# Two norms of a sum moved from VectorE to ScalarE, and the clamp in one pass, in the front stage of a two-layer megakernel

## The chip, the cores and the metric

One Trainium2 chip; the kernel is one program on one core. The metric is device time in microseconds, the median of several runs. The profile is of one execution.

## The reference, cut to what matters

The input x is 8192 tokens (8 x 1024) of 256 channels. The network is attention, a linear layer on values rounded to fp8, a Mamba-like mixer with an MLP, and a gated MLP, each behind a layer norm without weights. The part that the change touches is the second layer and the double norm behind it:

```python
x = x + _L0_attn_ref(_layernorm(x), ...)
# fp8 layer
n = _layernorm(x)
x_q = jnp.clip(n / input_scale, -448.0, 448.0)
x_dq = x_q.astype(jnp.float8_e4m3fn).astype(x.dtype) * input_scale
x = x + jnp.einsum('bsi,oi->bso', x_dq, weight_fp8 * weight_scale) + bias
# mixer: xc is the norm of x; inside, xc is normed again, then times ln1_w
xc = _layernorm(x)
h = layer_norm(xc, ln1_w)
xz = jnp.einsum('bld,ed->ble', h, in_proj_w)     # then a causal convolution of 4 taps,
                                                 # silu, x_proj, dt_proj, softplus, the scan
```

A norm of a norm is the same difference from the mean with another rate, so the kernel makes both from one pair of mean and variance.

## The kernel before, in words

Four stages run one behind the other: attention, the front stage (`front`), the mixer's scan, and the tail. The change is in `front`, which takes 625.5 us of the profiled execution. It holds the fp8 layer, both norms, the mixer's input projection, the convolution with its silu, and the projections to dt, B and C, and it stores all of that to HBM for the scan.

The tokens are cut into 16 groups of 512 (G = 4 tiles of 128 tokens). The stage is a software pipeline written out by hand. Each engine has a `body(i, k, s0..s5)`, and runs it for i = -1 to 19, the flags being the steps that have a group to work on: s0 is group i+1 (norm, rounding to fp8, product), s1 group i (sum, norms), s2 group i-1 (projection `project`, convolution), s3 group i-2 (`project_x`, `turn_b`, `project_dt`), s4 group i-3 (softplus and `dx`, turned by `turn_d`), s5 group i-4 (a store). Bodies 3 to 14 have all of s0 to s4. Every engine works through its queue in order, and engines meet only at semaphores.

The order of the work in a body, per engine:

- VectorE: `rate(i+1)` (mean and variance of the input); `add(i)` (x2 = product + bias + input, from PSUM, then its mean and variance); `quantize(i+1)` (norm, times 1/input_scale with an upper clamp, L1194, lower clamp, L1196, rounding to fp8 by adding and subtracting a magnitude, giving xq); `with_bias(i+1)`; `norms(i)`, which makes x3, the twice normed x2, and xc, the once normed x2; then four times `convolve(i-1, m)`, and after the second and fourth of them `sizes(i-3)`, which makes dt and dx (L1244, L1249).
- GpSimd: the two powers of -1/2, for `rstd` (group i+1) and `rstd2` (group i, both rates).
- ScalarE: `rows_copy`; a table load; `x_copy` 0 to 3 with the exponentials and logarithms (`power`, `log`) between them; a table load; `b_copy` (L1308); `parts` 0 (L1316, L1317); `z_silu` 0 and 1 (L1298); `parts` 1; `q_copy(i+1)` (L1332, the turned xq from PSUM to SBUF); `z_silu` 2 and 3; `l_copy(i)` (L1339, the turned x3); four `x_silu` (L1292); four `d_copy(i-3)` (L1347, the turned dx).
- TensorE: `project_x` (L1427); `project` 0 to 3 (L1418, the x half); `turn_b` (L1435); `project_dt` 0, 1 (L1444); `project` 4 and 5 (z half); `project_dt` 2, 3; turn of xq (L1399); `project` 6 and 7; turn of x3 (L1399, waits for `x3_ok`); `product(i+1)` (L1409); `turn_d` 0 to 3 (L1457). `turn_d` j for j > 1 waits until `d_copy` j-2 has emptied its half of the PSUM tile, and `project_x` waits for `d_copy` 2.
- SyncE: loads and stores, each behind a semaphore. The stores of x2 and xc (L1122, L1123) wait for `xc_ok`; behind them in the queue are the stores of dt, dx and bT, and the next body's load of x and its stores. `add` of the next group waits until the store of x2 has landed, since there is one buffer for x2.

`norm_apply` (L975) is four instructions of 128x256, one for each tile, with mean and rate as operands from memory:

```python
nc.vector.tensor_scalar(out[:, i, :], x[:, i, :], mv[:, i, 0:1], rstd[:, i:i + 1], ALU.subtract, ALU.mult)
```

Of the kernel before, what the change touches and what calls it, by code (L numbers as in the profile page):

```python
# [8 lines left out]
ACT = mybir.ActivationFunctionType  # L9
# [4 lines left out]
P = 128  # L14
# [17 lines left out]
def wait(eng, sem, value):  # L32

    if isinstance(value, int) and value <= 0:
        return
    eng.wait_ge(sem, value)
# [917 lines left out]
G = 4  # L954
# [17 lines left out]
def norm_apply(nc, dve, out, x, mv, rstd):  # L972

    for i in range(G):
        last = nc.vector.tensor_scalar(out[:, i, :], x[:, i, :], mv[:, i, 0:1], rstd[:, i:i + 1],  # L975
                                               ALU.subtract, ALU.mult)
    return last
# [10 lines left out]
def front(nc, x_in, w8, scales, col, bias, ident_in, x_out, xc_out, w_in_d, w_x_d, w_dt_d, cols_d, made):  # L988

    with ExitStack() as ctx:  # L990
        sb = lambda name, shape, dt=F32: ctx.enter_context(nc.sbuf_tensor(name, shape, dt))
        two = lambda name, shape, dt=F32: [sb(f"{name}{i}", shape, dt) for i in range(2)]
        sem = lambda name: ctx.enter_context(nc.semaphore(name))
# [9 lines left out]
        rs = sb("b_rs", [P, 1])  # L1003
# [5 lines left out]
        stats, stats2 = sb("b_stats", [P, G, 6]), sb("b_stats2", [P, G, 6])  # L1009
        mv, mv2 = sb("b_mv", [P, G, 2]), sb("b_mv2", [P, G, 2])  # L1010
        ve, ve2 = sb("b_ve", [P, G]), sb("b_ve2", [P, 2, G])
        rstd, rstd2 = sb("b_rstd", [P, G]), sb("b_rstd2", [P, 2, G])
        xn = sb("b_xn", [P, G, D])
        mag = sb("b_mag", [P, G, D])
# [2 lines left out]
        x2 = sb("b_x2", [P, G, D])  # L1017
        xc = sb("b_xc", [P, G, D])
        x3 = sb("b_x3", [P, G, D])
# [12 lines left out]
        x_in_s, x_free = sem("b_x_in"), sem("b_x_free")  # L1032
        a_step, ra_ok, b_step, rb_ok, q_step = (sem(f"b_{n}") for n in ("a_step", "ra_ok", "b_step", "rb_ok", "q_step"))
        xb_ok, xq_ok, x3_ok, xc_ok = sem("b_xb_ok"), sem("b_xq_ok"), sem("b_x3_ok"), sem("b_xc_ok")
        t_ok, t_free = sem("b_t_ok"), sem("b_t_free")
        y_ok, y_free = sem("b_y_ok"), sem("b_y_free")
        i_ok, i_free, c_ok, sx_ok = sem("b_i_ok"), sem("b_i_free"), sem("b_c_ok"), sem("b_sx_ok")
# [3 lines left out]
        st_x2, st_xc, st_sz, st_xv, st_dT, st_bc, st_bT, st_dt, st_dx = (  # L1041
            sem(f"b_st_{n}") for n in ("x2", "xc", "sz", "xv", "dT", "bc", "bT", "dt", "dx"))
# [18 lines left out]
        def first_use(g):  # L1061
            return 0 if isinstance(g, int) and g == 0 else 2 * g - 1
# [100 lines left out]
        def _(dve):  # L1163
# [21 lines left out]
            def rate(g, k):  # L1185
                dve.wait_ge(x_in_s, 16 * g + 16)
                sums(xt[k], stats, mv, a_step, 3 * g)
                nc.vector.tensor_scalar(ve[:].unsqueeze(2), mv[:, :, 1:2], LN_EPS, None, ALU.add).then_inc(a_step, 1)

            def quantize(g, k):  # L1190
                dve.wait_ge(ra_ok, g + 1)
                norm_apply(nc, dve, xn, xt[k], mv, rstd).then_inc(x_free, 1)
                dve.wait_ge(x_free, g + 1)
                nc.vector.tensor_scalar(xn[:], xn[:], rs[:, 0:1], 448.0, ALU.mult, ALU.min).then_inc(q_step, 1)  # L1194
                dve.wait_ge(q_step, 5 * g + 1)
                nc.vector.tensor_scalar(xn[:], xn[:], -448.0, None, ALU.max).then_inc(q_step, 1)  # L1196
                dve.wait_ge(q_step, 5 * g + 2)
                nc.vector.tensor_scalar(mag[:].bitcast(U32), xn[:].bitcast(U32), 0x7F800000, None,
                                        ALU.bitwise_and).then_inc(q_step, 1)
                dve.wait_ge(q_step, 5 * g + 3)  # L1200
                nc.vector.tensor_scalar(mag[:], mag[:], 2.0 ** -6, 1.5 * 2.0 ** 20, ALU.max, ALU.mult).then_inc(q_step, 1)
                dve.wait_ge(q_step, 5 * g + 4)
                nc.vector.tensor_tensor(xn[:], xn[:], mag[:], ALU.add).then_inc(q_step, 1)
                dve.wait_ge(q_step, 5 * g + 5)
                wait(dve, y_ok, 2 * g)
                nc.vector.tensor_tensor(xq[:], xn[:], mag[:], ALU.subtract).then_inc(xq_ok, 1)

            def add(g):
                dve.wait_ge(xb_ok, g + 1)
                dve.wait_ge(st_x2, 16 * g + 16)  # L1210
                for j in range(2):
                    dve.wait_ge(y_ok, 2 * g + j + 1)
                    nc.vector.tensor_tensor(x2[:, 2 * j:2 * j + 2, :], ps_y[j][:], xb[:, 2 * j:2 * j + 2, :],
                                            ALU.add).then_inc(y_free, 1)
                dve.wait_ge(y_free, 2 * g + 2 + 2)
                sums(x2, stats2, mv2, b_step, 4 * g)

                nc.vector.tensor_scalar(ve2[:, 0].unsqueeze(2), mv2[:, :, 1:2], LN_EPS, None, ALU.add).then_inc(b_step, 1)
                nc.vector.tensor_scalar(ve2[:, 1].unsqueeze(2), mv2[:, :, 1:2], 1.0 + LN_EPS, EPS2, ALU.mult, ALU.add
                                        ).then_inc(b_step, 1)  # L1220

            def norms(g):
                dve.wait_ge(rb_ok, g + 1)
                dve.wait_ge(t_ok, 4 * g + 2)
                norm_apply(nc, dve, x3, x2, mv2, rstd2[:, 1]).then_inc(x3_ok, 1)
                dve.wait_ge(st_xc, 16 * g + 16)
                norm_apply(nc, dve, xc, x2, mv2, rstd2[:, 0]).then_inc(xc_ok, 1)

            def convolve(g, k, m):
                dve.wait_ge(i_free, 8 * g + m + 1 + 2)  # L1230
# [20 lines left out]
            def with_bias(g, k):  # L1251
                dve.wait_ge(y_free, 2 * g + 2)
                nc.vector.tensor_tensor(xb[:], xt[k][:], b_row[:].broadcast_to([P, G, D]), ALU.add).then_inc(xb_ok, 1)

            def body(i, k, s0, s1, s2, s3, s4, s5):
                if s0:
                    rate(i + 1, 1 - k)
                if s1:
                    add(i)
                if s0:  # L1260
                    quantize(i + 1, 1 - k)
                    with_bias(i + 1, 1 - k)
                if s1:
                    norms(i)
                if s2:
                    for m in range(CH):
                        convolve(i - 1, 1 - k, m)
                        if s4 and m % 2:
                            sizes(i - 3, 1 - k, m // 2)
                elif s4:  # L1270
                    for h in range(2):
                        sizes(i - 3, 1 - k, h)

            loop(dve, body)

        @block.scalar
        def _(act):
# [51 lines left out]
            def q_copy(g):  # L1329
                for j in range(2):  # L1330
                    act.wait_ge(t_ok, 2 * first_use(g) + j + 1)
                    nc.scalar.activation(xT[:, j], ps_t[j][:], ACT.Copy, scale=sc[:, 0:1]).then_inc(t_free, 1)  # L1332

            def l_copy(g):
                wait(act, i_ok, 8 * g)
                for j in range(2):
                    act.wait_ge(t_ok, 2 * later_use(g) + j + 1)
                    for c in range(DC):
                        last = nc.scalar.activation(xl[:, c, 2 * j:2 * j + 2, :], ps_t[j][:, :, c, :], ACT.Copy,  # L1339
                                                    scale=ln_w[:, c:c + 1])  # L1340
                    last.then_inc(t_free, 1)
# [7 lines left out]
            def body(i, k, s0, s1, s2, s3, s4, s5):  # L1349
                k1 = 1 - k  # L1350
                if s3:
                    rows_copy(i - 2, k)
                if s4:
                    act.preload_act_table_set("natural_log_exp_and_others")
                for h in range(2):
                    if s2:
                        x_copy(i - 1, k1, 2 * h)
                    if s4:
                        power(i - 3, k1, h)
                    if s2:  # L1360
                        x_copy(i - 1, k1, 2 * h + 1)
                    if s4:
                        log(i - 3, k1, h)
                if s4:
                    act.preload_act_table_set("silu_and_others")
                if s3:
                    b_copy(i - 2, k)
                    parts(i - 2, k, 0)
                if s2:
                    z_silu(i - 1, k1, 0)  # L1370
                    z_silu(i - 1, k1, 1)
                if s3:
                    parts(i - 2, k, 1)
                if s0:
                    q_copy(i + 1)
                if s2:
                    z_silu(i - 1, k1, 2)
                    z_silu(i - 1, k1, 3)
                if s1:
                    l_copy(i)  # L1380
                if s2:
                    for m in range(CH):
                        x_silu(i - 1, k1, m)
                if s4:
                    for j in range(G):
                        d_copy(i - 3, k1, j)
# [775 lines left out]
```

## Time and profile before

| | |
|---|---|
| median of 3 timed runs | 6412.2 us (6410.86 to 6412.49) |
| profiled execution: its own time | 6411.39 us |
| its span in the trace | 6409.5 us |
| mean granted TensorE clock over the span | 0.957 of full speed |
| busy, share of the span: TensorE, VectorE, ScalarE, GpSimd | 86%, 73%, 69%, 58% |
| front stage, in the trace | 3199 to 3824.5 us |

Spans and starts are microseconds from the start of the trace. "Busy" leaves out waits and the issue of transfers. The clock is given as a share: 1.00 is 2.4 GHz and 0.50 is 1.2 GHz; a mean between the two is a mixture of stretches at either. A bracket behind a row of the timeline is how long the engine stood idle before it, and which instruction's end released it. Rows of equal instructions are merged (x4), and their time is that of all together. Instructions that follow directly on ScalarE or VectorE overlap by about 0.1 us, so the mean duration is longer than the distance from start to start.

### The profile page before, as it was taken

What the parts mean: (1) busy time and instruction counts of PE and PEld (TensorE: products, weight loads), DVE (VectorE), ACT (ScalarE), POOL (GpSimd) and SP (SyncE); (2) the same over time, 40 slices, a digit from 0 to 9 for tenths busy, and PEclk for the clock granted to TensorE, in tenths of its full rate; (3) what the DMA queues carried; (4) which work ended last, traced back from release to release, by engine and by line L of the source; (5) the groups of instructions that cost most, each with busy time, mean ns of one, the idle gap of its engine ahead of it and who ended that gap; (6) DMA issues with size and microseconds to landing.
All of it is one profiled execution on the core that took longest, in us unless ns stands there. A gap on an engine that the chain in (4) does not pass through costs nothing. (4 is left out here: it accounts for less than half of the span.)

```text
span 6409.5 us, 126137 instructions
## 1 busy us (share of the span) xinstructions
PE 5519.4 (86%) x40354; PEld 3585.7 (56%) x40354; DVE 4680.5 (73%) x6108; ACT 4439.7 (69%) x7115; POOL 3700.8 (58%) x2063
## 2 busy tenths in 40 slices
PE   3688888888888888888779968899989879999999
PEld 3466666666666666665534435445545446666665
DVE  1688888889888888888788949999999971221221
ACT  1698998989899898999846668888888851111111
POOL 2677777777777777777500009999999960000000
PEclk7899999999999999999989979999999989999999
DMA  1212111121211112120036555555555541111110
GB/s 34 43 27 46 29 38 34 27 46 29 43 28 33 40 29 43 28 45 18 16 125 216 203 202 187 201 194 182 202 179 203 198 153 46 33 33 49 33 33 10
DMA packets 470081, 538.36 MB, mean 84 GB/s; under 512 B 251056, under 2 KB 345008, under 8 KB 469568
## 3 DMA queue, kind: packets, MB, share of 16 engines
q1 hardware_dynamic: 469568, 531.63, 27.2%
q8 instruction: 309, 5.06, 0.3%
q14 instruction: 204, 1.67, 0.1%
HBM read 370.18 MB, written 161.35 MB: 83 GB/s over the span
## 5 line engine op out<-in xcount | busy, mean ns | idle before, releaser
L317 DVE CUSTOM_DVE_ANT_0 srow<-srow,ps_s,cur 128x1024 f32<-128x1024 f32 x1024 | 1304.0, 1273 | 267.9 <-PE ps_s L465 184.5
L394 ACT ACTIVATE srow<-srow,nmax 128x1024 f32<-128x1024 f32 x1024 | 1190.4, 1162 | 207.8 <-DVE nmax L317 195.4
L403 ACT COPY AT<-ps_t 128x512 f32<-128x512 f32 x2048 | 1104.9, 597 | 79.3 <-PE ps_t L476 78.3
L476 PEld LDWEIGHTS ps_t<-ident,srow 128*128 128x128 f32 x8192 | 965.6, 143 | 278.7 <-ACT AT L403 82.5
L476 PE MATMUL ps_t<-ident,srow 128*128 128x128 f32 x8192 | 1106.6, 279 | 12.6 <-ACT AT L403 8.5
L1725 POOL TENSOR_TENSOR c_hc<-c_hs,c_cs 128x1024 f32<-128x1024 f32 x432 | 1009.7, 2368 | 21.1 <-DVE c_hs L1826 19.3
L465 PE MATMUL ps_s<-K,Q 96*128 96x512 bf16 x2048 | 633.5, 392 | 440.4 <-DVE nmax L317 317.4
L306 DVE SCALAR_TENSOR_TENSOR srow<-ps_p,rho,R 128x1024 f32<-128x1024 f32 x768 | 975.4, 1270 | 13.7 <-ACT ps_p L357 9.2
L1686 PE MATMUL c_ps_y<-c_hc,c_ident 128*128 128x512 f32 x2048 | 956.6, 600 | 1.5
L1826 DVE TENSOR_TENSOR_SCAN c_hs<-c_da,c_pd 128x1024 f32<-128x1024 f32 x384 | 864.3, 2276 | 48.2 <-PE c_pd L1677 45.9
L1770 ACT ACTIVATE c_sT<-c_dxT,c_bT 128x256 f32<-128x256 f32 x1536 | 668.5, 494 | 141.3 <-PE c_pd L1677 131.6
L226 POOL TENSOR_TENSOR srow<-srow,R 128x1024 f32<-128x1024 f32 x256 | 611.6, 2389 | 47.0 <-POOL srow L224 47.0
L488 PE MATMUL ps_o<-AT,V 128*32 128x128 f32 x16384 | 621.8, 282 | 2.5 <-issue 2.5
L1677 PEld LDWEIGHTS c_pd<-c_ident,c_sT 128*128 128x128 f32 x3072 | 354.1, 142 | 404.1 <-issue 194.0
L1677 PE MATMUL c_pd<-c_ident,c_sT 128*128 128x128 f32 x3072 | 410.9, 278 | 161.1 <-DVE c_hc L1833 105.7
L1686 PEld LDWEIGHTS c_ps_y<-c_hc,c_ident 128*128 128x128 f32 x2048 | 363.5, 192 | 317.7 <-issue 308.9
L1964 POOL TENSOR_TENSOR d_rstd<-d_ve,d_mhalf 128x4 f32<-128x4 f32 x16 | 16.3, 1017 | 899.1 <-DVE d_ve L969 899.1
L465 PEld LDWEIGHTS ps_s<-K,Q 96*128 96x128 bf16 x2048 | 133.4, 98 | 660.7 <-DVE nmax L317 548.1
L488 PEld LDWEIGHTS ps_o<-AT,V 128*32 128x32 f32 x16384 | 409.6, 111 | 137.5 <-issue 134.1
L199 POOL TENSOR_TENSOR R<-Dj,RT 128x1024 f32<-128x1024 f32 x128 | 300.6, 2370 | 304.5 <-DVE RT L292 304.5
L1761 ACT ACTIVATE c_da<-c_dt,c_a_neg 128x1024 f32<-128x1024 f32 x384 | 435.8, 1135 | 0.0
L1718 POOL TENSOR_TENSOR c_db<-c_dx,c_bs 128x1024 f32<-128x1024 f32 x128 | 304.0, 2375 | 201.1 <-DMA c_bs<-bc_d 184.0
(196 smaller groups left out, 8364.7 us busy)
## 6 DMA issues: line engine op xcount, KB each, us to landing
c_cs<-bc_d SPq DMA_DIRECT2D x256, 512.0 KB, 4.2
c_bs<-bc_d SPq DMA_DIRECT2D x64, 512.0 KB, 4.7
parts_d<-parts SPq DMA_DIRECT2D x65, 384.0 KB, 3.3
K<-parts_d SPq DMA_DIRECT2D x192, 128.0 KB, 4.5
Q<-parts_d SPq DMA_DIRECT2D x384, 64.0 KB, 2.9
sz_d<-b_sz SPq DMA_DIRECT2D x16, 1024.0 KB, 7.2
xv_d<-b_xv SPq DMA_DIRECT2D x16, 1024.0 KB, 7.8
dt_d<-b_ab SPq DMA_DIRECT2D x16, 1024.0 KB, 4.2
```

What stands on the lines that cost most here:

```text
L306: nc.vector.scalar_tensor_tensor(r[:], ps_p[:], rho[:, h:h + 1], R[k][0][:], ALU.mult, ALU.add).then_inc(fd_ok, 1)
L317: nc.vector.tensor_tensor_reduce(r[:], r[:], ps_s[:], cur[k][:, h:h + 1], BIG, ALU.add, ALU.min, nmax[:, h % NROW:h % NROW + 1]).then_inc( ...
L394: nc.scalar.activation(r[:], r[:], ACT.Exp, scale=-1.0, bias=nmax[:, h % NROW:h % NROW + 1]).then_inc(e_ok, 1)
L403: nc.scalar.copy(AT[h % NAT][:, HG * half:HG * half + HG, :], ps_t[:, half]).then_inc(at_ok, 1)
L465: last = nc.tensor.matmul(ps_s[:, n * 512:(n + 1) * 512], Q6[k][:, h, :], K6[:, h, n * 512:(n + 1) * 512], start=True, stop=True)
L476: last = nc.tensor.transpose(ps_t[:, half, i, :], rows_sb[h % NROW][:, j * P:(j + 1) * P], ident[:])
L488: last = nc.tensor.matmul(ps_o[32 * i:32 * i + 32, j, :], V[par][:, n, h, :], AT[h % NAT][:, n, :], start=(n == 0), stop=(n == NT - 1))
L1677: last = nc.tensor.transpose(pd[:, c, k * P:(k + 1) * P], src[:, k, c * P:(c + 1) * P], ident[:])
L1686: last = nc.tensor.matmul(ps_y[:, c, cut], ident[:], hc[place((n, c)) % NHC][:, cut], start=n == 0, stop=n == NS - 1)
L1725: nc.gpsimd.tensor_tensor(hc[place((n, c)) % NHC][:], hs[place((n, c)) % NHS][:], cs[n % NCS][:], ALU.mult).then_inc(hp_ok, 1)
L1770: last = nc.scalar.activation(sT[i % NSC][:, k, :], dxT[p][:, k, :], ACT.Copy, scale=bT[p][:, k, n:n + 1])
L1826: nc.vector.tensor_tensor_scan(h, gain, push, 0.0, ALU.mult, ALU.add).then_inc(h_ok, 1)
```

## The change

`norms` leaves VectorE. VectorE instead computes, in `offsets`, the product of the negated mean and each rate (two instructions of 128x4 into the new tile `shift`), and ScalarE applies both norms as an activation Identity with `scale` = rate and `bias` = shift, four instructions of 128x256 for x3 and four for xc. In ScalarE's queue they stand between `q_copy` and `z_silu` 2. The new semaphore `sh_ok` tells ScalarE that shift is ready, and `xc_ok` is now counted by ScalarE.

In `quantize`, 1/input_scale (`rs`) is multiplied into the rate `rstd` (128x4) ahead of the norm, and the two passes over 128x1024 that scaled and clamped become one that clamps at both ends.

```diff
+        shift = sb("b_shift", [P, 2, G])
+        sh_ok = sem("b_sh_ok")
...
             def quantize(g, k):
                 dve.wait_ge(ra_ok, g + 1)
+                nc.vector.tensor_scalar(rstd[:], rstd[:], rs[:, 0:1], None, ALU.mult).then_inc(q_step, 1)
+                dve.wait_ge(q_step, 5 * g + 1)
                 norm_apply(nc, dve, xn, xt[k], mv, rstd).then_inc(x_free, 1)
                 dve.wait_ge(x_free, g + 1)
-                nc.vector.tensor_scalar(xn[:], xn[:], rs[:, 0:1], 448.0, ALU.mult, ALU.min).then_inc(q_step, 1)
-                dve.wait_ge(q_step, 5 * g + 1)
-                nc.vector.tensor_scalar(xn[:], xn[:], -448.0, None, ALU.max).then_inc(q_step, 1)
+                nc.vector.tensor_scalar(xn[:], xn[:], 448.0, -448.0, ALU.min, ALU.max).then_inc(q_step, 1)
...
-            def norms(g):
+            def offsets(g):
                 dve.wait_ge(rb_ok, g + 1)
-                dve.wait_ge(t_ok, 4 * g + 2)
-                norm_apply(nc, dve, x3, x2, mv2, rstd2[:, 1]).then_inc(x3_ok, 1)
-                dve.wait_ge(st_xc, 16 * g + 16)
-                norm_apply(nc, dve, xc, x2, mv2, rstd2[:, 0]).then_inc(xc_ok, 1)
+                wait(dve, xc_ok, g)
+                for n in range(2):
+                    last = nc.vector.scalar_tensor_tensor(shift[:, n].unsqueeze(2), mv2[:, :, 0:1], -1.0,
+                                                          rstd2[:, n].unsqueeze(2), ALU.mult, ALU.mult)
+                last.then_inc(sh_ok, 1)
...
                 if s1:
-                    norms(i)
+                    offsets(i)
...
+            def norm(g, out, n, done):
+                for j in range(G):
+                    last = nc.scalar.activation(out[:, j, :], x2[:, j, :], ACT.Identity, bias=shift[:, n, j:j + 1],
+                                                scale=rstd2[:, n, j:j + 1])
+                last.then_inc(done, 1)
+
+            def norms(g):
+                act.wait_ge(sh_ok, g + 1)
+                act.wait_ge(t_ok, 4 * g + 2)
+                norm(g, x3, 1, x3_ok)
+                act.wait_ge(st_xc, 16 * g + 16)
+                norm(g, xc, 0, xc_ok)
...
                 if s0:
                     q_copy(i + 1)
+                if s1:
+                    norms(i)
                 if s2:
                     z_silu(i - 1, k1, 2)
                     z_silu(i - 1, k1, 3)
```

## Rows read from the trace of the kernel before

**Rows 1.** Windows, the front stage: span, busy us (instructions) by engine, PEclk, DMA share

```profile
3199.00:3824.50 625.50, 522.79 (x1664) 260.62 (x1664) 496.17 (x966) 369.56 (x545) 46.65 (x33) 0.88 0.51 180
```

**Rows 2.** The same view for two loop bodies, from product to product

```profile
3503.71:3537.30 33.59, 31.39 (x106) 15.70 (x105) 29.82 (x56) 22.88 (x35) 2.94 (x2) 0.95 0.54 193
...
3639.60:3674.35 34.75, 32.55 (x107) 16.12 (x106) 31.79 (x64) 22.88 (x35) 2.94 (x2) 0.90 0.59 211
```

**Rows 3.** Timeline, one body, TensorE and ScalarE: start, us, engine, line, out<-in, [idle before<-releaser]

```profile
3523.77 1.12 PE L1444 MATMUL b_ps_m<-b_bc,b_w_dt 17*128 17x512 f32 x2 [1.71 <-ACT b_bT L1308]
...
3532.17 1.03 ACT L1316 ACTIVATE b_ab<-b_ps_m 128x1024 f32<-128x1024 f32 x1 [1.31 <-PE b_ps_m L1444]
...
3533.99 1.27 ACT L1332 ACTIVATE b_xT<-b_ps_t,b_sc 128x512 f32<-128x512 f32 x2
...
3535.13 0.62 ACT L1298 ACTIVATE b_sz<-b_ps_i 128x512 f32<-128x512 f32 x1
...
3536.43 1.04 PE L1399 MATMUL b_ps_t<-b_ident,b_x 128*128 128x128 f32 x8
...
3536.63 0.60 ACT L1298 ACTIVATE b_sz<-b_ps_i 128x512 f32<-128x512 f32 x1 [0.88 <-PE b_ps_i L1418]
...
3538.54 2.57 ACT L1292 ACTIVATE b_xv<-b_xd,b_cols 128x512 f32<-128x512 f32 x4
...
3540.76 1.04 PE L1457 MATMUL b_ps_m<-b_ident,b_dx 128*128 128x128 f32 x8
...
3541.39 1.07 ACT L1347 COPY b_dT<-b_ps_m 128x512 f32<-128x512 f32 x2 [0.28 <-PE b_ps_m L1457]
...
3542.03 1.15 PE L1457 MATMUL b_ps_m<-b_ident,b_dx 128*128 128x128 f32 x8 [0.24 <-ACT b_dT L1347]
```

**Rows 4.** Timeline of the same body, VectorE

```profile
3518.23 1.38 DVE L975 TENSOR_SCALAR b_x<-b_x,b_mv,b_rstd 128x256 f32<-128x256 f32 x4
...
3535.57 1.23 DVE L1249 TENSOR_TENSOR b_dx<-b_ab,b_xv 128x1024 f32<-128x1024 f32 x1
...
3539.23 0.69 DVE L1213 TENSOR_TENSOR b_x<-b_ps_y,b_xb 128x512 f32<-128x512 f32 x1 [0.37 <-PE b_ps_y L1409]
```

**Rows 5.** Timeline, second body: the store of x2, and who waits for it

```profile
3244.54 0.38 SPq L1122 DMA_DIRECT2D x_d<-b_x  x1
...
3248.85 1.29 DVE L1213 TENSOR_TENSOR b_x<-b_ps_y,b_xb 128x512 f32<-128x512 f32 x2 [2.36 <-DMA x_d<-b_x]
```

**Rows 6.** Instruction groups by form in 3250 to 3700 us: busy, mean ns

```profile
L1298 ACT ACTIVATE b_sz<-b_ps_i 128x512 f32<-128x512 f32 x53 | 31.9, 601 | 49.6 <-PE b_ps_i L1418 49.6
...
L1332 ACT ACTIVATE b_xT<-b_ps_t,b_sc 128x512 f32<-128x512 f32 x26 | 16.5, 692 | 0.0
...
L1194 DVE TENSOR_SCALAR b_xn<-b_xn,b_rs 128x1024 f32<-128x1024 f32 x14 | 10.5, 753 | 0.5
...
L1196 DVE TENSOR_SCALAR b_xn<-b_xn 128x1024 f32<-128x1024 f32 x14 | 9.7, 695 | 0.5
...
L1188 DVE TENSOR_SCALAR b_ve<-b_mv 128x4 f32<-128x4 f32 x13 | 2.2, 170 | 0.4
```

**Rows 7.** ScalarE in the mixer: the group on the page, and three in the timeline

```profile
L1770 ACT ACTIVATE c_sT<-c_dxT,c_bT 128x256 f32<-128x256 f32 x1536 | 668.5, 494 | 141.3 <-PE c_pd L1677 131.6
...
4300.44 1.29 ACT L1770 ACTIVATE c_sT<-c_dxT,c_bT 128x256 f32<-128x256 f32 x3
```

**Rows 8.** Timeline of TensorE: a long wait at that place, and the usual body

```profile
3336.11 1.14 PE L1457 MATMUL b_ps_m<-b_ident,b_dx 128*128 128x128 f32 x8 [2.02 <-ACT b_dT L1347]
3337.61 5.33 PE L1427 MATMUL b_ps_m<-b_xv,b_w_x 128*48 128x512 f32 x8 [0.37 <-ACT b_dT L1347]
...
3543.54 3.63 PE L1427 MATMUL b_ps_m<-b_xv,b_w_x 128*48 128x512 f32 x8 [0.36 <-ACT b_dT L1347]
```

**Rows 9.** Timeline: TensorE in the first bodies, ScalarE in the last with norms

```profile
3240.77 1.97 PE L1399 MATMUL b_ps_t<-b_ident,b_xq 128*128 128x128 f32 x8 [9.81 <-DVE b_xq L1206]
...
3741.03 0.60 ACT L1298 ACTIVATE b_sz<-b_ps_i 128x512 f32<-128x512 f32 x1 [1.12 <-PE b_ps_i L1418]
```

## The prediction, made before the changed kernel was run

> **What bounds the kernel now.** The windows by stage come first: the front stage spans 625.5 us, with TensorE busy for 522.8, VectorE 496.2 and ScalarE 369.6 [rows 1]. By these shares TensorE and VectorE are both near their limit and ScalarE has room, which is what makes moving norms to ScalarE tempting. A share does not say whose lateness moves the end, so next I read single loop bodies, from the start of one product to the next [rows 2]: 33.59 us in some, 34.75 us in others, ScalarE busy for 22.9 us in both, the difference being TensorE's granted clock (0.95 against 0.90 in the mean).
>
> Then the timeline of one body [rows 3]. TensorE runs back to back except at two places, and both wait for ScalarE. (1) The dt projections wait 1.71 us for the small copy of B, which stands behind `log` and a table load. (2) The second half of `turn_d` (3542.03) starts right after ScalarE's `d_copy` (3541.39). Ahead of that copy ScalarE has only 0.88 us of idle before `z_silu` 3 and 0.28 us before `d_copy`, since the moment when it started after `q_copy` at 3535.13. Upstream, ScalarE's `parts` (3532.17) wait for TensorE. So from 3532 to 3542 the two engines run nearly level, and from 3542 on TensorE carries the ring alone into the next body.
>
> VectorE, in contrast, has slack [rows 4]. It makes x3 at 3518.23, and TensorE turns it at 3536.43, some 16 us later. It ends the last `dx` at 3536.8, and `turn_d` wants it at 3540.76: 4 us of slack. It then waits 0.37 us for the product itself. Its busy 29.8 of 33.6 us is high [rows 2], but in the steady bodies nobody waits for it.
>
> **The change, part by part.** *Clamp.* Of the two passes L1194 (0.753 us) and L1196 (0.695) one is left, with two immediates, which I price like L1196; added is a multiply of 128x4 like L1188 (0.170) [rows 6]. With some 0.04 us of gap each, 0.58 us per group is freed.
>
> *Norms off VectorE.* Eight instructions go, four in 1.38 us [rows 4]: 2.6 to 2.8 us. Two small ones of 128x4 come (0.17 each, by L1188), so 2.4 us are freed. Together VectorE is 3.0 us lighter per body. In steady bodies this is worth nothing, as above: it lengthens VectorE's wait for the product. In the first bodies it is worth something: TensorE waits 9.81 us for xq at 3240.77 [rows 9], behind VectorE's chain. Following those bodies with VectorE 0.58 us (twice) and then 3 us lighter per body, and ScalarE 3.9 us heavier, I get TensorE some 1.0 us early at the second half of `turn_d` of body 3. I take −1.0, bounds −2.5 and +2.
>
> *Norms on ScalarE.* Eight Identity activations of 128x256 from SBUF with a pointer for scale and one for bias. No row has both. With one pointer and the same shape and memory, one takes 0.494 us alone and three take 1.29, so 0.40 from start to start [rows 7]. A scale pointer costs 0.692 − 0.601 = 0.091 us [rows 6] (L1332 against L1298, PSUM, 512 wide). So 0.49 each, 3.92 us for eight. The lower bound is 0.40 (a second pointer free, 3.2 us), the upper 0.58 (0.494 + 0.091 with no overlap, 4.7 us).
>
> *Where they stand.* They sit in ScalarE's queue between `q_copy` and `z_silu` 2. Behind them are `z_silu` 2 and 3, `l_copy`, four `x_silu` and `d_copy`, and TensorE waits for the last. Before: `d_copy` at 3541.39. After, in the same frame [rows 3]: norms from 3535.13 to 3539.05; `z_silu` 3 0.52 later; from its start to that of the first `x_silu` 1.91 (3536.63 to 3538.54, back to back); `x_silu` 2.57 less about 0.1 of overlap; `d_copy` at 3543.95. That is +2.56 us: of 3.92, 1.36 go into the idle time of ScalarE. TensorE meets it twice: x3 is ready only at 3535.13 + 3 × 0.49 + 0.58 + 0.1 = 3537.3 instead of early, so its turn at 3536.43 slips by 0.85 us; that moves the product and the first half of `turn_d` (3540.76 + 1.04) to end at 3542.65, and the second half can start only at 3544.6. TensorE stands idle there for 1.9 us; the 0.85 us is inside the 2.56, not beside it.
>
> *Eleven bodies* (groups 4 to 14) have all of this: 11 × 2.56 = 28.2 us. The body of group 15 has norms but no `q_copy` and no product; ScalarE idles 1.12 us ahead of `z_silu` 3 there [rows 9], so 3.92 − 1.2 = 2.7 us.
>
> *The clock.* A wait of 2.02 us for the same copy is in the trace already, in the fourth body [rows 8]: behind it the eight matmuls of L1427 take 5.33 us where the usual body has 3.63. I read it as the clock falling to its lower level behind the idle stretch: +1.70 us. The wait of 1.71 us for B is followed by such a stretch too, and the bodies of 34.75 us are those where it lasts twice as long [rows 2]: 1.2 us more. A wait of 0.24 us at that place leaves 3.63 [rows 3, 8]. I expect the 1.9 us to act like the 2.02: 11 × 1.70 = 18.7 us. Bounds: 0, and 1.70 + 1.2 = 2.9 a body, 32 us.
>
> *The stores.* x2 and xc are stored once ScalarE is done (about 3539.1 instead of 3521). SyncE's queue waits there, with the stores of dt, dx and bT and the next load behind. From store to the next `add` into x2 was 4.3 us in the second body, where VectorE did wait for it [rows 5]. So `add` moves from 3539.23 to about 3543.6, 4.4 us late; ring later by 2.6, VectorE lighter by 3.0 and with 4 us of slack [rows 4]: nothing is added. If the store took over 8 us, this cover would be gone. In the second body it delays `add` by some 2 us, which is in the −1.0. The dt store slips 4 us, its buffer is wanted more than a body later.
>
> **Sum** against the profiled execution's 6411.4 us (span 6409.5 and 1.9 around it; the median of the three timed runs is 6412.2, 0.8 above): −1.0 + 28.2 + 2.7 + 18.7 = +48.6, so 6460.0 us, 0.75% slower.
>
> **A rule of the skill.** The bargain as such: eight norms cost VectorE 2.8 us [rows 4] and ScalarE 3.9 by the rows above. The Trainium skill, "ScalarE: Activation LUTs", section "Rules for kernel authors", says to do plain adds and multiplies on VectorE rather than ScalarE. The trace agrees for this shape, 0.34 against an estimated 0.49 us; it would speak against the change even were the queues equal.
>
> **Rivals.**
> *A: the clock does not fall.* The new wait may be shared out differently from the 2.02 us one, and only the shift remains: 6411.4 + 29.9 = 6441 us. For it: 1.9 is below 2.02. Against it: 1.71 us of waiting is followed by the lower clock in the bodies of rows 2 and 3. 10%.
> *B: VectorE sets the body after all* and the result is faster. Its busy share and the first bodies speak for it; if steady bodies were tied to it, 16 × 3.0 = 48 us would go: 6363 us. It decides if VectorE's waits for the product (0.37 us) are the exception. Against it: the 16 us between x3 and its use, and the 4 us at `dx` [rows 4]. 4%.
> *C: the extra work is hidden.* ScalarE idles 10.7 us in a body [rows 2]; if its order let the norms fall into that, only the first bodies' effect stays: 6410, no change. Its queue is in order, and just 1.4 us of the idle lies between `q_copy` and `d_copy`. 5%.
> *D: a table load around Identity.* If Identity is not in the loaded table, two loads a body join the ring. Such a load stands between `log` and the copy of B and is part of that wait of 1.71 us [rows 3], so two of them bring at most 3.4 us to a body: 12 bodies, up to 41 us more, at most 6501. 4%. The Trainium skill, "ScalarE: Activation LUTs", section "Table sets: the hidden batching unit", lists identity among the cheap functions in every set; by that, no load appears. No run so far shows it.
> *The forecast, with the lower clock lasting once or twice*: 77%.
>
> **How the numbers follow.** Within the forecast, cheap norms (0.40) give 11 × 1.84 + 2.0 − 1.0 + 18.7 = +40, 6451; dear ones (0.58) with falls of 2.9 give 11 × 3.3 + 3.4 − 1.0 + 32 = +71, 6482. Rival A reaches to 6441, and with cheap norms to 6433. The range is 6438 to 6481. What a measurement here can tell from no change is about 0.2%, 13 us. Slower by more holds the forecast, A and D: 0.91; within it is C: 0.05; faster is B: 0.04.
>
> **What would show it.** In the profile after: the ScalarE group of the norms at 128x256 with a mean near 0.58 and no idle inside; idle of TensorE at L1457's successor waiting for the copy to dT near 1.9 us, 13 times; a new wait of TensorE for x3 near 0.8; L1427's successor at 5.3 instead of 3.6; bodies of 37.5 to 39.5 us; VectorE waiting for the store or the product, 3 us more per body; ScalarE busy 26.8 us a body; no more table loads than two a body. The prediction is wrong if the wait for dT is short, which would mean that norms cost less than half of 0.49 or that the ring runs elsewhere; or if L1427's successor stays at 3.6, which is A.

## The result, and the profile after

| | before | after |
|---|---|---|
| median | 6411.5 us (6406.8 to 6412.5, 4 runs) | 6448.1 us (6444.0 to 6451.0, 4 runs) |
| profiled execution, own time | 6411.4 us | 6450.1 us |
| its span | 6409.5 us | 6448.3 us |

The changed kernel is slower by 0.58% (ratio 1.0058, 95% interval 1.0041 to 1.0075), 36.6 us between the medians. The prediction was 6460 with a range of 6438 to 6481.

The whole loss lies in the front stage. Measured from VectorE's first instruction in the stage to ScalarE's table load at the head of the mixer, it takes 623.2 us before (3201.31 to 3824.55) and 665.4 after (3197.72 to 3863.13): +42.2. Attention, which is the same code, ended 3.6 us earlier in this execution, so that the spans differ by 38.8 only. The stage in the windows view of the changed kernel (span, then busy time of TensorE, its weight loads, VectorE, ScalarE and GpSimd, the granted clock, the DMA share):

```profile
3199.00:3860.00 661.00, 538.33 (x1664) 263.86 (x1664) 447.21 (x866) 427.12 (x672) 49.58 (x32) 0.87 0.48 169
```

VectorE is busy 49 us less than in [rows 1], ScalarE 58 us more. Two bodies, from product to product, in the same view:

```profile
3516.00:3553.34 37.34, 32.93 (x106) 16.04 (x105) 27.83 (x54) 26.53 (x43) 3.15 (x2) 0.91 0.52 185
3553.34:3591.10 37.76, 33.11 (x107) 15.94 (x105) 27.92 (x54) 26.59 (x43) 3.15 (x2) 0.91 0.51 183
```

They answer to [rows 2]: 37.3 and 37.8 us instead of 33.6 and 34.8, ScalarE 26.5 instead of 22.9, VectorE 27.9 instead of 29.8 and 31.8. The granted clock is lower in the mean, not higher. The timeline of one body, TensorE and ScalarE, to be laid beside [rows 3]:

```profile
3501.48 1.12 PE L1462 MATMUL b_ps_m<-b_bc,b_w_dt 17*128 17x512 f32 x2 [1.71 <-ACT b_bT L1311]
...
3509.87 1.03 ACT L1319 ACTIVATE b_ab<-b_ps_m 128x1024 f32<-128x1024 f32 x1 [1.31 <-PE b_ps_m L1462]
...
3511.70 1.27 ACT L1335 ACTIVATE b_xT<-b_ps_t,b_sc 128x512 f32<-128x512 f32 x2
...
3512.84 2.07 ACT L1339 ACTIVATE b_x<-b_x,b_shift,b_rstd 128x256 f32<-128x256 f32 x4
...
3514.80 2.08 ACT L1339 ACTIVATE b_xc<-b_x,b_shift,b_rstd 128x256 f32<-128x256 f32 x4
...
3515.07 1.09 PE L1417 MATMUL b_ps_t<-b_ident,b_x 128*128 128x128 f32 x8 [0.78 <-ACT b_x L1339]
...
3516.77 1.07 ACT L1301 ACTIVATE b_sz<-b_ps_i 128x512 f32<-128x512 f32 x2
...
3519.15 2.58 ACT L1295 ACTIVATE b_xv<-b_xd,b_cols 128x512 f32<-128x512 f32 x4
...
3519.45 1.04 PE L1475 MATMUL b_ps_m<-b_ident,b_dx 128*128 128x128 f32 x8
...
3521.60 1.09 ACT L1363 COPY b_dT<-b_ps_m 128x512 f32<-128x512 f32 x2
...
3522.26 1.15 PE L1475 MATMUL b_ps_m<-b_ident,b_dx 128*128 128x128 f32 x8 [1.77 <-ACT b_dT L1363]
...
3523.67 3.63 PE L1445 MATMUL b_ps_m<-b_xv,b_w_x 128*48 128x512 f32 x8 [0.26 <-ACT b_dT L1363]
```

Read it downwards. `parts` (3509.87) wait for TensorE as before, `q_copy` follows, and then the norms take 3512.84 to 3516.77, 3.93 us for eight. TensorE wants x3 and waits 0.78 us. `z_silu` 2 and 3 now run back to back (1.07 us for two), so that the idle time between them is used up. `d_copy` starts at 3521.60, and TensorE, which has been through with the first half of `turn_d` since 3520.49, starts the second half after 1.77 us of waiting. The norms by themselves, and their durations (minimum, median, maximum in ns):

```profile
L1339 ACT ACTIVATE b_x<-b_x,b_shift,b_rstd x64: 587/607/617, 3239.6 to 3775.9; 128x256 f32<-128x256 f32 x64
L1339 ACT ACTIVATE b_xc<-b_x,b_shift,b_rstd x64: 590/599/608, 3241.6 to 3777.8; 128x256 f32<-128x256 f32 x64
```

VectorE and the store of x2 in the same body:

```profile
3511.80 0.17 DVE L1190 TENSOR_SCALAR b_ve<-b_mv 128x4 f32<-128x4 f32 x1
...
3517.15 0.38 SPq L1124 DMA_DIRECT2D x_d<-b_x  x1
...
3520.40 1.29 DVE L1215 TENSOR_TENSOR b_x<-b_ps_y,b_xb 128x512 f32<-128x512 f32 x2 [8.44 <-DMA x_d<-b_x]
```

VectorE has its last power operand ready at 3511.97 and then waits 8.44 us for the store of x2, issued only at 3517.15. That looks alarming, and TensorE does not wait for VectorE anywhere in the steady bodies (ScalarE does four times, for 0.2 us each). The clock behind the two waits, TensorE alone:

```profile
3484.53 1.15 PE L1475 MATMUL b_ps_m<-b_ident,b_dx 128*128 128x128 f32 x8 [1.80 <-ACT b_dT L1363]
3486.03 5.15 PE L1445 MATMUL b_ps_m<-b_xv,b_w_x 128*48 128x512 f32 x8 [0.36 <-ACT b_dT L1363]
...
3502.53 5.40 PE L1436 MATMUL b_ps_i<-b_xl,b_w_i 128*128 128x512 f32 x8
...
3537.52 2.07 PE L1462 MATMUL b_ps_m<-b_bc,b_w_dt 17*128 17x512 f32 x2 [1.63 <-ACT b_bT L1311]
3539.52 5.78 PE L1436 MATMUL b_ps_i<-b_xl,b_w_i 128*128 128x512 f32 x8
```

In one body `project_x` (L1445) takes 5.15 us behind the wait for dT, in the next 3.63 (the last two rows of the timeline above), though the waits are nearly the same, 1.80 and 1.77 us. There the projections behind the wait for B take longer instead (5.78 for eight against 5.40). Read in windows of half a microsecond over eleven steady bodies, from the product of group 5 on, TensorE stands at the lower level (1.2 GHz) for 54.6 us before and for 75 us after. Low stretches come single, at a cost of 1.7 us, or double; counted single, there are 16 before, all behind the wait for B, five of those falls being double. After, there are 22: seven behind the wait for dT, and 15 behind the wait for B, four of those falls being double.

The first bodies, to be laid beside [rows 5, 8, 9], TensorE:

```profile
3241.75 1.97 PE L1417 MATMUL b_ps_t<-b_ident,b_x 128*128 128x128 f32 x8 [2.74 <-ACT b_x L1339]
...
3333.72 1.14 PE L1475 MATMUL b_ps_m<-b_ident,b_dx 128*128 128x128 f32 x8 [1.87 <-ACT b_dT L1363]
3335.23 5.33 PE L1445 MATMUL b_ps_m<-b_xv,b_w_x 128*48 128x512 f32 x8 [0.37 <-ACT b_dT L1363]
```

VectorE, the first instruction of the stage and the wait for the store of x2:

```profile
3197.72 0.07 DVE L1166 MEMSET b_xpad<- 128x12 f32 x1 [2.28 <-PEq L61]
...
3247.76 0.69 DVE L1215 TENSOR_TENSOR b_x<-b_ps_y,b_xb 128x512 f32<-128x512 f32 x1 [7.44 <-DMA x_d<-b_x]
```

### The profile page after: what moved, and what is told of

It is laid out like the page before. It is cut to its first block and busy times, and to the rows that moved or that the text cites. A ratio compares the mean times of both kernels' runs of the same rounds, so it can differ in the third digit from the quotient of the medians.

```text
span 6448.3 us, 126194 instructions
## 1 busy us (share of the span) xinstructions
PE 5533.6 (86%) x40354; PEld 3588.9 (56%) x40354; DVE 4633.5 (72%) x6012; ACT 4498.4 (70%) x7243; POOL 3703.6 (57%) x2063
```

## The experiments

A steady body is given as the mean over the ten from the product of group 5 to that of group 15, from the profiled execution; low stretches are counted over the eleven bodies named above, a double one as two, and divided by eleven. "Front stage" is measured as above.

| kernel | median, and that of before measured with it | ratio (95%) | front stage | steady body | low stretches a body |
|---|---|---|---|---|---|
| before | 6411.5 | | 623.2 | 34.1 | 1.5 |
| the change | 6448.1, 6411.5 | 1.0058 (1.0041 to 1.0075) | 665.4 | 37.6 | 2.0 |
| e1 clamp only | 6402.6, 6406.9 | 0.9989 (0.9980 to 0.9999) | 617.7 | 34.1 | 1.4 |
| e2 eight idle norms | 6447.9, 6406.9 | 1.0069 (1.0056 to 1.0083) | 663.9 | 37.5 | 2.0 |
| e3 filler | 6445.6, 6406.9 | 1.0066 (1.0052 to 1.0079) | 664.5 | 37.5 | 2.0 |
| e4 norms at another place | 6394.4, 6406.9 | 0.9983 (0.9974 to 0.9992) | 617.7 | 34.2 | 1.5 |
| e5 four idle norms | 6408.6, 6409.1 | 0.9998 (0.9988 to 1.0007) | 621.3 | 34.1 | 1.0 |
| e6 six idle norms | 6430.4, 6409.1 | 1.0032 (1.0020 to 1.0045) | 648.2 | 36.2 | 1.6 |
| e7 early copy of B | 6377.0, 6409.1 | 0.9947 (0.9931 to 0.9964) | 590.0 | 31.9 | 0.5 |
| e8 e4 and e7 | 6360.2, 6409.1 | 0.9913 (0.9897 to 0.9930) | 574.6 | 31.1 | 0.2 |
| e9 e7 and the clamp | 6368.1, 6407.4 | 0.9941 (0.9925 to 0.9958) | 584.5 | 31.4 | 0.3 |
| e10 change and early copy | 6397.7, 6407.4 | 0.9985 (0.9975 to 0.9994) | 614.5 | 34.1 | 1.0 |

### e1: the clamp alone

```diff
--- before
+++ e1: quantize as in the change, norms(i) as before
-                nc.vector.tensor_scalar(xn[:], xn[:], rs[:, 0:1], 448.0, ALU.mult, ALU.min).then_inc(q_step, 1)
-                nc.vector.tensor_scalar(xn[:], xn[:], -448.0, None, ALU.max).then_inc(q_step, 1)
+                nc.vector.tensor_scalar(rstd[:], rstd[:], rs[:, 0:1], None, ALU.mult).then_inc(q_step, 1)
...
+                nc.vector.tensor_scalar(xn[:], xn[:], 448.0, -448.0, ALU.min, ALU.max).then_inc(q_step, 1)
```

> The kernel before with only the one-pass clamp; both norms stay on VectorE. Theory (the ring of a steady body runs over TensorE and ScalarE, VectorE has some 4 us of slack): VectorE busy 0.6 us less per body, bodies of group 4 to 14 unchanged, only the first bodies up to 2 us earlier; total 6410 to 6412 us. Rival (VectorE's time sets the body): 16 x 0.6 = 9 us faster, 6402.

The steady body stays at 34.1 us, which is the theory's point. The total is 4 us lower, more than the 2 us forecast for the first bodies and half of the rival's 9. In the profile the product of group 1 comes 2.0 us earlier after the start of the stage (41.7 against 43.7), and the fifth body is 35.4 us instead of 38.1; the theory's bound of 2 us was too tight there, since in the first bodies a gain on VectorE is passed on to the next. The interval ends at 0.9999, so the gain in the median is hardly clear of the noise.

### e2: the norms' time on ScalarE, with nothing moved

```diff
--- before
+++ e2
                 if s0:
                     q_copy(i + 1)
+                if s1:
+                    wait(act, sp_ok, i)
+                    for n in range(8):
+                        last = nc.scalar.activation(spare[:, n, :], w_i[:, 0, 0:D], ACT.Identity, bias=ln_w[:, 0:1],
+                                                    scale=sc[:, 0:1])
+                    last.then_inc(sp_ok, 1)
```

> The kernel before, norms and clamp as they were on VectorE, plus eight Identity activations of 128x256 with two pointers in ScalarE's queue between q_copy and z_silu 2, on constant inputs into a tile that nobody reads. Nothing waits for their result. Theory (the loss is the length of ScalarE's queue between parts and d_copy, and its clock): body longer by 2.5 to 2.7 us and part of the falls behind the wait for dT; front stage longer by 36 to 43 us, total 6447 to 6454, the same as the changed kernel within 4 us; no wait of TensorE for x3. Rival (the loss comes from the hand-over: x3 late at TensorE, the late store of x2, VectorE's wait for it): total near 6412 to 6420.

VectorE does all of its old work here, x3 is early, x2 is stored early, and the kernel is as slow as the changed one: 6447.9 against 6448.1 us, 41 and 37 us above their own runs of before (the intervals of the ratios overlap), body 37.5 against 37.6. So the loss is the 3.9 us in ScalarE's queue at that place, not the hand-over. (What the hand-over costs in the first bodies and what the lighter VectorE gives back there about cancel: the two front stages differ by 1.5 us.) TensorE in a steady body:

```profile
3521.26 1.28 PE L1465 MATMUL b_ps_m<-b_ident,b_dx 128*128 128x128 f32 x8 [2.76 <-ACT b_dT L1349]
3522.67 5.04 PE L1435 MATMUL b_ps_m<-b_xv,b_w_x 128*48 128x512 f32 x8
```

There is no wait for x3, and the wait for dT is 2.76 us instead of 0.24. What the changed kernel has in two waits, 0.78 and 1.77 us, is here in one piece, and the difference of 2.52 us is the shift that was forecast as 2.56.

### e3: the wait filled, against the clock

```diff
--- after
+++ e3: turn_d
-                for m in range(CH):
-                    last = nc.tensor.transpose(ps_m[:, j % 2, ...], dx[k][:, m, ...], ident[:])
+                for _ in range(4 if j == 1 else 1):
+                    for m in range(CH):
+                        last = nc.tensor.transpose(ps_m[:, j % 2, ...], dx[k][:, m, ...], ident[:])
```

> The changed kernel, with TensorE doing the transposes of turn_d 1 four times instead of once, so that some 1.35 us of its wait of 1.8 us for the copy to dT are filled with matmuls nobody needs. Theory (about 10 us of the 42 us are the clock's lower level behind this wait): none of the seven low stretches behind the wait is left, project_x always 3.6 us; shift of 2.6 us a body remains; total 6448 minus 5 to 12, so 6436 to 6443. Rival (the falls only trade places with the doubled ones behind the wait for B): low time unchanged, total 6446 to 6452. Second rival (the extra transposes delay d_copy 1): longer than 6452.

TensorE in e3, `turn_d` 2 and 3, `project_x`, and the matmuls behind the wait for B:

```profile
3512.93 1.15 PE L1476 MATMUL b_ps_m<-b_ident,b_dx 128*128 128x128 f32 x8 [0.46 <-ACT b_dT L1363]
3514.34 3.63 PE L1445 MATMUL b_ps_m<-b_xv,b_w_x 128*48 128x512 f32 x8 [0.26 <-ACT b_dT L1363]
...
3528.18 2.07 PE L1462 MATMUL b_ps_m<-b_bc,b_w_dt 17*128 17x512 f32 x2 [1.63 <-ACT b_bT L1311]
```

The filler does what it should: the wait shrinks to 0.46 us and `project_x` takes 3.63 us in every steady body. And the body stays at 37.5 us. Every fall behind the wait for B is double now: 22 low stretches in eleven bodies, as many as in the changed kernel. The rival of this run was right: the falls changed places. Its total, 2.5 us below the changed kernel's median, is within what the two sets of runs can tell. So the seven falls behind the wait for dT can't be called its price; the price that the runs show is that of the whole body.

### e4: the same norms at another place in the queue

```diff
--- after
+++ e4: ScalarE's body
+                early = s1 and s3
+                if early:
+                    norm_x3(i)
                 if s2:
                     z_silu(i - 1, k1, 0)
+                if early:
+                    norm_xc(i)
+                if s2:
                     z_silu(i - 1, k1, 1)
...
-                if s1:
-                    norms(i)
+                if s1 and not early:
+                    norm_x3(i)
+                    norm_xc(i)
```

> The changed kernel with the norms at another place of ScalarE's queue: from body 2 on, x3 before z_silu 0 and xc before z_silu 1, where ScalarE stood idle for 1.0, 1.7 and 1.3 us. Theory (place, not amount, makes the loss): no wait of TensorE for x3, wait for the copy to dT back at 0.24 us, bodies of 33.6 to 34.9 us as before the change, total 6408 to 6416. Rival (ScalarE's total of 26.9 us is what costs, or z_silu 0 and 1 now hold up the projections): total 6425 to 6450.

Same instructions, same total on ScalarE, and the loss is gone: 6394.4 us, 54 below the changed kernel's median (48 us in the front stage) and faster than before the change (ratio 0.9983). ScalarE between the two `parts`, and TensorE at `turn_d`:

```profile
3514.16 1.02 ACT L1320 ACTIVATE b_rl<-b_ps_m 128x1024 f32<-128x1024 f32 x1
...
3515.06 2.07 ACT L1339 ACTIVATE b_x<-b_x,b_shift,b_rstd 128x256 f32<-128x256 f32 x4
...
3517.03 0.58 ACT L1301 ACTIVATE b_sz<-b_ps_i 128x512 f32<-128x512 f32 x1
...
3517.51 2.07 ACT L1339 ACTIVATE b_xc<-b_x,b_shift,b_rstd 128x256 f32<-128x256 f32 x4
...
3519.47 0.58 ACT L1301 ACTIVATE b_sz<-b_ps_i 128x512 f32<-128x512 f32 x1
...
3520.66 1.03 ACT L1319 ACTIVATE b_ab<-b_ps_m 128x1024 f32<-128x1024 f32 x1 [0.60 <-PE b_ps_m L1471]
```

And the second half of `turn_d`:

```profile
3495.88 1.15 PE L1484 MATMUL b_ps_m<-b_ident,b_dx 128*128 128x128 f32 x8 [0.24 <-ACT b_dT L1365]
3497.28 3.63 PE L1454 MATMUL b_ps_m<-b_xv,b_w_x 128*48 128x512 f32 x8 [0.26 <-ACT b_dT L1365]
```

The norms (3515.06, 3517.51) stand where ScalarE used to wait for the slow projections, `parts` 1 still has 0.60 us of idle in front, and TensorE's wait for dT is back at 0.24 us. The theory's 6408 was too high: with VectorE lighter and the hand-over early, the first bodies gain, as they were meant to in the prediction (the products of groups 4 and 5 come at 125.6 and 159.4 us after the start instead of 127.3 and 165.5). That gain is mostly the clamp's: e1, which has the clamp alone, has the same front stage of 617.7 us, and the intervals of e1 and e4 overlap. So at this place the norms cost nothing, but no gain from having them off VectorE is shown.

### e5 and e6: four and six idle norms

As e2, with `range(4)` and `range(6)`.

> As e2, the kernel before plus idle Identity activations behind q_copy, but four instead of eight: 1.96 us, of which 1.36 go into ScalarE's idle time. Six kernels so far show only two mean lengths of a steady body, 34.1 and 37.5 us, whatever stands in the ring. Theory S (body lengths go in steps, since single and doubled low stretches of the clock take turns so as to fill up a longer step): mean body stays 34.1, total within 3 us of before. Rival (a plain sum): 0.6 us a body, 34.7, total 7 us above before.

> The same with six: 2.94 us, 1.58 beyond ScalarE's idle time. Theory S: the body doesn't fit the shorter step any more and goes to 37.5, as with eight; total 35 to 41 us above before. Rival (a plain sum): 34.1 + 1.6 and at most 1.7 for a fall behind the wait for dT: 35.7 to 37.4, total 19 us above before if that wait of 1.8 us lets the clock fall in half of the bodies or less.

TensorE in e5, `turn_d`, `project_x` and the projections behind the wait for B:

```profile
3494.63 1.14 PE L1465 MATMUL b_ps_m<-b_ident,b_dx 128*128 128x128 f32 x8 [0.81 <-ACT b_dT L1349]
3496.03 3.63 PE L1435 MATMUL b_ps_m<-b_xv,b_w_x 128*48 128x512 f32 x8 [0.27 <-ACT b_dT L1349]
...
3509.96 1.22 PE L1452 MATMUL b_ps_m<-b_bc,b_w_dt 17*128 17x512 f32 x2 [1.71 <-ACT b_bT L1310]
```

TensorE in e6, two bodies:

```profile
3475.90 1.14 PE L1465 MATMUL b_ps_m<-b_ident,b_dx 128*128 128x128 f32 x8 [1.78 <-ACT b_dT L1349]
3477.41 3.63 PE L1435 MATMUL b_ps_m<-b_xv,b_w_x 128*48 128x512 f32 x8 [0.36 <-ACT b_dT L1349]
...
3511.09 1.14 PE L1465 MATMUL b_ps_m<-b_ident,b_dx 128*128 128x128 f32 x8 [1.78 <-ACT b_dT L1349]
3512.50 5.31 PE L1435 MATMUL b_ps_m<-b_xv,b_w_x 128*48 128x512 f32 x8 [0.26 <-ACT b_dT L1349]
```

With four, the wait for dT grows by 0.57 us, as the sum has it (0.81 against 0.24), and the body is 34.1 us as before: there is no double fall left (10 low stretches in 10 bodies instead of 16 in 11), and that pays for the 0.6. With six, theory S falls: 36.2 us, between the two values, 21 us above before, near the 19 of the plain sum. Waits for dT of 1.78 us are followed by `project_x` of 3.63 in one body and of 5.31 in the next, in the same kernel. So body lengths do not go in steps in general; what holds over e2, e3, e5 and e6 is that low stretches change their places and their number when a wait is added, so that a small one can cost nothing and a bigger one more than itself.

### e7 to e10: the other wait of TensorE

```diff
--- before
+++ e7: ScalarE's body
                     if s2:
                         x_copy(i - 1, k1, 2 * h + 1)
+                    if s3 and h == 1:
+                        b_copy(i - 2, k)
                     if s4:
                         log(i - 3, k1, h)
...
                 if s3:
-                    b_copy(i - 2, k)
                     parts(i - 2, k, 0)
```

> The kernel before, norms on VectorE, with the small copy of B moved ahead of the second log and the table load on ScalarE. Theory: TensorE's wait for it falls from 1.7 to 0.3 us and with it the clock's lower level in steady bodies; TensorE's ring would be 30.1 us, now below what VectorE needs (29.9 to 31 us busy), so VectorE sets the body: 31 to 31.8 us, total 25 to 35 us below before, and TensorE waits for VectorE. Rival (parts behind log and table load now come late, dt 2 and 3 wait in turn): 10 us or less below before.

> e4 and e7 together: norms on ScalarE ahead of z_silu 0 and z_silu 1, and the copy of B early. Theory: VectorE is 3 us lighter, so TensorE and ScalarE set the body at 30.1 to 30.8 us; total 45 to 60 us below before, 10 to 25 below e7. Rival (ScalarE, 26.9 us busy of 30.5, has no idle left between parts and z_silu 0 now, and the norms there push everything as they did in the changed kernel): no better than e7.

e7 gives 32 us and e8 49 us. The wait for B is gone and with it most of the low clock: 5 low stretches in e7 and 2 in e8 over eleven bodies. TensorE and ScalarE in a body of e7:

```profile
3441.63 1.53 PE L1445 MATMUL b_ps_m<-b_bc,b_w_dt 17*128 17x512 f32 x3
3441.78 0.21 ACT L1308 COPY b_bT<-b_ps_m 128x64 f32<-128x64 f32 x1 [0.39 <-PE b_ps_m L1436]
...
3457.64 2.56 ACT L1292 ACTIVATE b_xv<-b_xd,b_cols 128x512 f32<-128x512 f32 x4 [2.38 <-DVE b_dx L1249]
...
3460.72 1.14 PE L1458 MATMUL b_ps_m<-b_ident,b_dx 128*128 128x128 f32 x8 [2.10 <-ACT b_dT L1347]
3462.23 3.63 PE L1428 MATMUL b_ps_m<-b_xv,b_w_x 128*48 128x512 f32 x8 [0.36 <-ACT b_dT L1347]
```

The dt projections (3441.63) no longer wait. ScalarE's `x_silu` now waits 2.38 us for VectorE's dx, so `d_copy` is late and TensorE waits 2.10 us for dT. Five of the bodies 4 to 14 have such a wait of 2.0 to 2.1 us; behind two of them `project_x` takes 5.28 us, behind three, as here, 3.63. The windows view over 300 us of e8, columns as above:

```profile
3360.00:3660.00 300.00, 291.83 (x994) 144.81 (x995) 270.91 (x519) 252.36 (x402) 30.15 (x19) 0.99 0.61 219
```

The same for e7:

```profile
3360.00:3660.00 300.00, 284.76 (x978) 143.86 (x977) 287.49 (x570) 211.80 (x318) 29.15 (x20) 0.97 0.61 220
```

In e7 VectorE is busy for 287.5 of 300 us, and only now does its time decide. In e8 VectorE is busy for 270.9 us of a stretch that holds more bodies (9.7 instead of 9.4), and e8 is 17 us faster by the medians. ScalarE is busy for 252 of 300 us there, but from `parts` 0 to the first `d_copy` (3466.93 to 3482.55 us in one body) it has no idle time left.

> e7 (copy of B early, norms on VectorE) with the one-pass clamp. Theory (once TensorE's wait for B is gone, VectorE sets the body, so that its work counts one for one): 0.6 us less a body than e7, mean body 31.0 to 31.5 against 31.9, total 7 to 12 us below e7. Rival (VectorE still does not count, e8 gained by something else): within 3 us of e7.

> The changed kernel, norms between q_copy and z_silu 2, with the copy of B early. Theory (the place of the norms lengthens the ring by 2.5 us whatever the other waits do): mean body 32.6 us, or 34.4 if the wait of 1.8 us for dT lets the clock fall in every body; total 25 to 55 us below the changed kernel, and 18 to 45 above e8. Rival (with the copy early the place no longer matters): within 8 us of e8.

In e9 the clamp brings the body from 31.9 to 31.4 us, close to the 0.6 us that it takes off VectorE, where it brought nothing in e1; but e9 also has two low stretches fewer than e7 in its eleven bodies, which may be part of it. The medians put e9 9 us below e7, the ratios to before (0.9941 and 0.9947) 4 us; the latter is weaker than the forecast, and the intervals overlap. e8 has this clamp too, so that the norms' own part in its 17 us is what lies between e9 and e8: 8 us by the medians, 10 in the front stage, with intervals that just overlap. e10 puts the place of the norms to the test once more: 34.1 us a body against 31.1 in e8, 37.5 us by the medians, within the forecast. TensorE in e10:

```profile
3502.25 1.15 PE L1476 MATMUL b_ps_m<-b_ident,b_dx 128*128 128x128 f32 x8 [1.77 <-ACT b_dT L1363]
3503.66 5.20 PE L1446 MATMUL b_ps_m<-b_xv,b_w_x 128*48 128x512 f32 x8 [0.26 <-ACT b_dT L1363]
```

The wait for dT is 1.77 us as in the changed kernel, but here the clock falls behind it in each of the ten bodies. That there is no fall behind a wait for B to change places with is not the reason by itself: e7 has no such wait either, and three of its five long waits for dT are followed by full clock.

## Why the prediction was right, and where a term was off

**The mechanism was right.** The norms sit in ScalarE's queue between `parts` and `d_copy`, and TensorE waits for `d_copy`. e2 shows it with nothing else changed, e4 and e10 by moving the norms alone.

**The cost of eight norms.** Forecast 3.92 us with 0.49 from start to start; measured 3.93. The bound 0.58 was never near; the second pointer added what the first had, and the single instruction's mean of 0.60 us would mislead as the price of one in a row.

**The shift of a body.** Forecast 2.56 us, with waits of 0.85 for x3 and 1.9 for dT; measured waits 0.78 and 1.77. From the second half of `turn_d` in body 3 to that in body 14 the changed kernel takes 413.7 us, before 376.5: +37.2. In between there are 22 low stretches instead of 16; six at 1.7 us are 10.2, and the rest is 27.0, 2.5 a body. Forecast: 28.2.

**The clock, the term that was off.** "I expect the 1.9 us to act like the 2.02: 11 × 1.70 = 18.7 us." Six low stretches came on top, not eleven, 10 us. The step that failed is that falls behind the two waits add up. Four of the eleven waits for dT are followed by full clock, and the double falls behind the wait for B went from five to four. e3 shows that they are not independent: without any fall behind dT all of those behind B are double. What decides whether a wait is followed by the lower clock, and whether the fall is single or double, was not tried by itself and stays open.

**The first bodies.** Forecast −1.0 us at the second half of `turn_d` in body 3; measured +1.2 (136.0 against 134.8 us after the stage's start). VectorE's relief is there, but TensorE waits 2.74 us for x3 in the first body with norms (0.46 before), and the late store of x2 holds VectorE for 7.44 us in the next (2.36 before, [rows 5]). I had put the store at 2 us. e4, with the store early in all but the first two bodies, has its `turn_d` at 130.4 us, e1 at 132.0.

**The last body with norms.** Forecast 2.7; measured 36.4 against 33.5 us, 2.9. Behind it 0.8 us more, from slower matmuls behind a wait of 5.3 us.

**The sum.** 1.2 + 37.2 + 2.9 + 0.8 = 42.1 in the stage, against 48.6. The profiled executions differ by 38.8 in all, since attention took 3.6 us longer in that of before; the 36.6 of the medians is another 2 us lower, which is within the spread of the runs. Of the 12 us by which the median stays below the forecast, 8.5 are the clock; the other terms of the stage add 2, and the rest is attention and that spread, which no one forecast.

**The rivals.** A (no fall of the clock, 6441) lies nearer to the median, 7 us below it, than the forecast, 12 us above, but it is not what happened: the clock did take 10 us. The median alone could not have told the two apart. B (VectorE sets the body) is refuted for this kernel by e1 and e2, and becomes true in e7, as soon as TensorE's wait for B is gone. C (hidden) did not happen at this place; e4 shows that it needed another place, not less work. D (table loads): none appeared. By the Trainium skill, "ScalarE: Activation LUTs", section "Table sets: the hidden batching unit", identity is in every set, and the trace agrees: between `q_copy` and `z_silu` there are only the norms, and the table loads in the stage are as many as before.

The VectorE part of the forecast held too: e2 leaves VectorE as busy as before, and no difference from the changed kernel is clear of the noise.

**The slack at dx, a reading that was off.** The prediction gives VectorE 4 us, from the end of dx to `turn_d`. The first to wait for dx is ScalarE's `x_silu` 0, which overwrites a factor of it: it starts 1.74 us after dx ends (3536.80 and 3538.54, [rows 3, 4]), and the distance is 1.7 to 3.1 us in the steady bodies before. This did no harm here, since `x_silu` moved later and VectorE grew lighter. It is the wait through which VectorE sets the body in e7.

## What to carry to other kernels

Before moving work to an engine with a low busy share, find the stretch of its queue between the wait that it ends and the one that it causes: only the idle time inside that stretch is free. Here that was 1.4 us of 10.7, and three to four slots further up the same instructions cost nothing. A wait of the matmul engine has a second price in its clock, and this price is to be counted over the whole body, since falls move from one wait to another; removing the other wait of the body (e7, one line moved, 32 us) was worth more than the clamp and the norms at their best place (e4, 12 us).

## What the runs showed of the hardware that was not expected

Low stretches of TensorE's clock changed places without changing their number: two a body whether the wait for dT was 1.77 us, 2.76 us (e2) or filled down to 0.46 us (e3). Equal waits of 1.78 us in one kernel (e6) were followed by either level, and so were waits of 2.0 to 2.1 us in e7, which has few low stretches at all (5 in eleven bodies). Steady bodies came out at 34.1 or 34.2 us in five kernels and at 37.5 or 37.6 in three, though their waits for dT differ by up to 2.3 us; e6 at 36.2 shows that other lengths occur.
